# Moving the last two attention gate steps and one MLP group's norm work between pipeline turns

## The reference

```
x  = mobius_add(x, expmap0(g_msa * logmap0(attn_out)))     # the attention gate step
xm = expmap0(layer_norm(logmap0(x)) * (1 + sc_mlp) + sh_mlp)
ff = plin(plin(xm, w_f1, b_f1), w_f2, b_f2)
y  = mobius_add(x, expmap0(g_mlp * logmap0(ff)))           # the MLP gate step
out = x0 + mx_quantize(y) @ dequant(weight).T + bias       # groups of 32, FP6
```

## Time and profile before

| what | value |
|---|---|
| median of 3 runs | 1152.47 us (1149.03 to 1152.67) |
| profiled execution: its own time / its span | 1151.27 us / 1149.4 us |
| busy share of the span: PE, DVE, ACT, POOL | 87%, 84%, 74%, 48% |
| granted TensorE clock, mean over the span | 0.949 |
| loads of scale and shift rows, issue to landing (median) | 4.8 us and 5.9 us |
| first and last turn of the MLP loop touched by the change | from about 858 us to about 918 us |

### The profile page before, as it was taken

The page is one execution under the profiler, slowest core; times in us unless marked ns, Lnnn a source line. Parts: engine busy times, 40 slices in busy tenths (PEclk is TensorE's granted clock), DMA queues, the critical chain, the costliest instruction groups (busy, mean ns, idle before and its releaser), DMA issues.

```text
span 1149.4 us, 23488 instructions
## 1 busy us (share of the span) xinstructions
PE 999.6 (87%) x7666; PEld 647.6 (56%) x7688; DVE 964.9 (84%) x2211; ACT 854.4 (74%) x2322; POOL 551.0 (48%) x1009
## 2 busy tenths in 40 slices
PE   7999987887699279999999999999885688889876
PEld 7888873333355146666666666666552355455544
DVE  5888777999488867899998999999878799999983
ACT  3545548887797246888888888888778888888872
POOL 2344424554387432444444444444204576677763
PEclk9999998999599689999999999999997799999998
DMA  7111201341699643454554444442373555766634
GB/s 245 46 49 55 61 22 63 127 171 79 215 354 326 186 109 93 111 124 123 131 127 123 113 111 111 112 112 69 83 176 68 101 130 147 183 157 165 156 95 125
DMA packets 113676, 148.16 MB, mean 129 GB/s; under 512 B 9232, under 2 KB 99472, under 8 KB 112784
## 3 DMA queue, kind: packets, MB, share of 16 engines
q1 hardware_dynamic: 113008, 146.64, 46.8%
q10 hardware_dynamic: 544, 0.00, 0.0%
HBM read 111.22 MB, written 27.00 MB: 120 GB/s over the span
## 4 chain that ended last, share of the span: by engine, by line
PE 22%; issue 12%; ACT 12%; DVE 7%; POOL 6%; DMA 4%; SPq 2%; DVEq 0%; POOLq 0%; ACTq 0%
PE t_fB L2053 6%; POOL t_qk L1971 4%; PE t_bk L2022 4%; PE t_fA L2053 3%; PE t_bk L1386 3%; DMA t_qbd<-t_qt 3%; PE t_fB L1407 2%; SPq L1856 2%; ACT t_ysq L2192 1%; ACT t_junk L1425 1%; ACT t_vbd L1467 1%; ACT t_vbd L1451 1%; DVE t_qt L1619 1%; PE t_bk L2103 1%; ACT t_qt L2306 1%
## 5 line engine op out<-in xcount | busy, mean ns | idle before, releaser
L1386 PE MATMUL t_bk<-k_w12g,t_ut 128*128 128x512 f32 x256 | 126.3, 617 | 3.2 <-DVE t_y L1589 2.4
L412 POOL TENSOR_SCALAR s_hleak<-k_hs,k_leak 128x128 f32<-128x128 f32 x126 | 46.9, 372 | 96.2 <-ACT k_hs L367 96.2
L2053 PE MATMUL t_fA<-k_wqkv,t_ut 128*128 128x512 f32 (+1 forms) x256 | 91.2, 499 | 1.5 <-ACT t_ut L2162 1.5
L2053 PE MATMUL t_fB<-k_wqkv,t_ut 128*128 128x512 f32 (+1 forms) x256 | 90.9, 498 | 0.0
L285 PE MATMUL s_gsum<-k_hs,k_w0t 128*128 128x128 f32 x504 | 77.6, 297 | 6.8 <-ACT k_hs L367 0.8
L2022 PEld LDWEIGHTS t_bk<-t_qbd,t_kpar 64*128 64x128 f32 x1024 | 62.8, 189 | 31.6 <-ACT t_pt L2198 10.7
L2022 PE MATMUL t_bk<-t_qbd,t_kpar 64*128 64x128 f32 x1024 | 75.2, 287 | 6.2 <-DMA t_qbd<-t_qt 1.8
L1386 PEld LDWEIGHTS t_bk<-k_w12g,t_ut 128*128 128x128 f32 x256 | 50.4, 198 | 53.3 <-issue 49.6
L745 ACT ACTIVATE a_silu<-a_pg,k_wxscale 128x512 f32<-128x512 f32 x96 | 64.9, 694 | 17.5 <-PE a_pu L710 17.3
L285 PEld LDWEIGHTS s_gsum<-k_hs,k_w0t 128*128 128x128 f32 x504 | 65.6, 190 | 20.6 <-ACT k_hs L367 20.1
L364 ACT ACTIVATE s_gate<-s_gsum,k_b 128x128 f32<-128x128 f32 x128 | 40.1, 363 | 45.7 <-PE s_gsum L285 45.7
(11 more groups left out here) (388 smaller groups left out, 2910.1 us busy)
## 6 DMA issues: line engine op xcount, KB each, us to landing
t_scb<-g_rows SPq DMA_DIRECT2D x64, 256.0 KB, 4.8
t_shb<-g_rows SPq DMA_DIRECT2D x64, 256.0 KB, 5.9
hidden_rows<-k_own SPq DMA_DIRECT2D x6, 1536.0 KB, 6.0
t_qbd<-x_rows SPq DMA_DIRECT2D x17, 512.0 KB, 6.3
s_xrow<-in_x_dram SPq DMA_DIRECT2D x16, 512.0 KB, 3.6
b_xin<-in_x_dram SPq DMA_DIRECT2D x16, 512.0 KB, 4.5
x_rows<-b_xout SPq DMA_DIRECT2D x16, 512.0 KB, 6.6
t_xf<-x_rows SPq DMA_DIRECT2D x16, 512.0 KB, 5.6
```

Source lines behind the costliest of these rows:

```text
L1386: last = nc.tensor.matmul(z.fW[:, j, :], z.ut[:, c, j * P:(j + 1) * P], k["w12g"][:, c, :], start=False, stop=(c == C - 1))
L2053: last = nc.tensor.matmul(dst[:, w0:w1], ut[:, c, j * P:(j + 1) * P], k["wqkv"][:, c, w0:w1], start=(c == 0), stop=(c == C - 1))
```

## The change

On DVE, ACT and POOL the calls are put into another order; PE and SP are as before, and no instruction is added or taken away. The attention gate step of group 15 is issued in turn 4 on ACT and DVE (only its `gated` on DVE stays in turn 3) and at the end of turn 3 on POOL. The DVE part of group 14's step (`moved`, `moments`) goes from turn 2 to turn 3, and `squares_yo` of group 15 with POOL's `scaled_y(NG)` from turn 2 (on POOL from ahead of the loop) to turn 3. MLP group 2 has `norms_u` and `scaled_u` issued earlier in turn 2 on ACT, with `clip_u(2)` ahead of `scaled_norms(0)` on POOL and `modulate(2)`, `shift(2)` ahead of `gated(0)` on DVE. In turns other than 2, ACT's `norms_a` of the MLP stands ahead of the attention gate's `scaled_a`.

```diff
@@ POOL
             gate_step(NG)
-            scaled_y(NG)
             for i in range(NG + 4):
+                if i == 2:
+                    once(second.clip_u, 2)
                 once(second.scaled_norms, i - 2)
                 once(second.products, i - 4)
                 once(second.clip_u, i)
@@
                 once(second.quotients, i - 3)
                 once(second.factors, i - 2)
-                if i == 2:
+                if i == 3:
+                    scaled_y(NG)
                     scaled_norms(NG - 1)
+                once(second.clip_y, i - 1)
+                if i == 3:
                     gate_step(NG + 1)
-                once(second.clip_y, i - 1)
@@ ACT
-            gates = {2: turn(NG), 3: turn(NG + 1)}
+            gates = {2: turn(NG), 4: turn(NG + 1)}
@@
                 once(second.turned_u, i - 1)
                 if i in gates:
                     gates[i]["tanh_parts"]()
+                if i == 3:
+                    gates[2]["squares_yo"](NG)
+                once(second.norms_y, i - 2)
                 if i == 2:
-                    gates[i]["squares_yo"](NG)
-                once(second.norms_y, i - 2)
+                    once(second.norms_u, 2)
                 if i in gates:
                     gates[i]["inverse"]()
+                if i == 2:
+                    once(second.scaled_u, 2)
+                else:
+                    once(second.norms_a, i - 2)
+                if i in gates:
                     gates[i]["scaled_a"]()
                 once(second.norms_a, i - 2)
                 once(second.scaled_a, i - 3)
@@ DVE
-            gates = {2: turn(NG), 3: turn(NG + 1)}
+            gates = {2: turn(NG), 4: turn(NG + 1)}
@@
-                if i == 3:
-                    gates[i]["gated"]()
                 once(second.quads, i - 2)
                 once(second.moved, i - 4)
                 once(second.norm, i)
                 once(second.maxima, i - 4)
                 once(second.outer, i - 2)
+                if i == 2:
+                    once(second.modulate, 2)
+                    once(second.shift, 2)
                 once(second.gated, i - 2)
+                if i == 3:
+                    gates[2]["moved"]()
+                    gates[2]["moments"]()
+                    gates[4]["gated"]()
                 once(second.modulate, i)
                 once(second.shift, i)
-                if i in gates:
+                if i == 4:
                     gates[i]["moved"]()
                     gates[i]["moments"]()
                 once(second.gate_sums, i - 2)
```

## The result

| | before | after |
|---|---|---|
| median of 5 runs | 1152.67 us (1149.03 to 1153.08) | 1160.57 us (1158.23 to 1162.48) |
| profiled execution / span | 1151.27 / 1149.4 us | 1162.48 / 1160.7 us |
| `norm(2)` to `norm(5)` on DVE | 862.63 to 920.64: 58.01 us | 862.09 to 929.50: 67.41 us |
| from `norm(5)` to the end | 228.8 us | 231.2 us |

The changed kernel takes 1.0072 of the time before (95% interval 1.0050 to 1.0093), that is 8.3 us more. The forecast was 1161.0.

What follows compares the result with a forecast made beforehand. DVE was taken as the pace: its waits in turns 2 to 4 would grow from 8.2 to 17.1 us, 8.9 more, taking the profiled 1151.27 to 1160.2; with 1.2 for the median, the forecast was 1161.0, range 1154 to 1167.

Steps and rivals of the forecast that it cites:

- DVE is the pace: Settled MLP turn: DVE works 16.17 of 17 us, so what it loses at the transition is never caught up.
- Turn 2: DVE waits 1.6 us at quads(1) and 4.5 at outer(1) for root_quad(1), 6.1 instead of 3.8.
- Turn 3: ACT waits 1.9 us before inverse(0) for POOL's denominator; DVE runs through without a wait.
- Turn 4: Group 15: ACT waits 5.3 us before tanh_parts, 3.1 before inverse; DVE waits 11.0 at moved, starting 918.3.
- The two knots: POOL, Turn 4: scaled_norms behind quotients(0) and factors(1), gate step behind clip_y(2); ACT waits 5.3 and 3.1 us.
- The sum: DVE's waits in turns 2 to 4 total 17.1 us against 8.2, so 8.9 us more.
- The cost of a late `wide(4)`: PE may end wide(4) 0.5 to 1 us after DVE asks; offset by quads(3), so taken as nothing.
- slow-PE rival: After PE's long gap, wide(4) runs wholly at the lower clock: 6.6 us on top, 1167; 12 in 100.
- The bounds: On the 8.9 us loss: 6.1 without POOL stalls in turn 4, 0.5 without both knots; upwards, a slow PE.
- The lower bound of 0.5 us: If both POOL knots in turn 4 cost ACT nothing, the loss is 8.4 us less, 0.5.
- The 2.8 for a POOL without stalls: If DVE does not stall POOL's small instructions in turn 4, the loss is 2.8 us less, 6.1.
- The faster case: ACT's stops are filled, DVE waits under 2.1 us at group 15's moved: 2.1 us less, 1149.2; 6 in 100.

Runs made afterwards that it cites:

- before_filled: Kernel before, gates in old turns: DVE's gate_sums ahead of attention moved in turns 2 and 3, ACT's root_quad(1) and norms_a(1) earlier in turn 3; ratio 0.9999.
- both_knots: Changed kernel with POOL's scaled_y and scaled_norms of group 15 ahead of quotients(0), its gate step ahead of clip_y(2); ratio to before 1.0034.
- gate_sums_first: Changed kernel with DVE's gate_sums(2) ahead of modulate(4) and shift(4) in turn 4; ratio to the kernel before 1.0042.
- regrouped: Changed kernel with POOL as in both_knots, root_quad(1), root_quad(2), turned_u(2), norms_a(2), group 14's scaled_a earlier on ACT, gate_sums(2) earlier on DVE; ratio to before 1.0021.
- filled_and_freed: before_filled with POOL's scaled_norms of group 15 ahead of factors(0) in turn 2; ratio to the kernel before 0.9986 (0.9971 to 1.0002).
- before_dve_part: Kernel before with only DVE's gate_sums moved ahead of the attention moved in turns 2 and 3; ratio 1.0004.

## Why the prediction was right, point by point

- **DVE is the pace.** Right. The table's two columns are the evidence: stretches from -2.3 to +10.7 us come back in the times. The DVE half of before_filled marks the limit: `gate_sums` in DVE's own waits won nothing that can be seen (stretch -0.3): 1.2 us were won in turn 2, and most of that went into an instruction of DVE that now met a long one of POOL.
- **Turn 2.** `scaled_u(2)` started at 873.71 (873.7 foretold), `tanh_parts(0)` at 879.41 (879.45). DVE's stop was foretold as 1.6 at `quads(1)` and 4.5 at `outer(1)`, 6.1; it was 6.64, all at `outer(1)`. PE ran `wide(1)` at the full clock this time and had its last tile by 872.5, where the earlier trace rows have 874.7; the end, 881.2, is the same, because ACT sets it.
- **Turn 3.** ACT's wait before `inverse(0)`: 1.5 for 1.9. Nothing else waits, as written. The later loads of the gate rows cost nothing: no DMA is in the list of waits.
- **Turn 4.** Foretold and measured: ACT 5.3 and 5.5, then 3.1 and 3.2; `moved` at 918.3 and 918.16; DVE's wait 11.0 and 11.1. The two knots were then undone one at a time and gave back 5.1 and 3.1.
- **The sum.** 8.9 us forecast (as a time, 1160.2 and 1.2 make 1161.4, not the 1161.0 written); the profiled stretch grew by 9.4 and the timed difference is 8.3 (5.8 to 10.7). The cost of a late `wide(4)`, taken as nothing against the wait that falls away at `quads(3)`, was fair: `quads(3)` and `quads(4)` follow each other by 15.4 us, with no wait. The list in the earlier trace rows ends at 918; at 918.45 DVE waited 0.57 us in `quads(3)` for the last tile of `wide(3)`, so the slow products of the old order did cost DVE something, against what the slow-PE rival says. That is the wait that falls away.
- **The bounds.** The lower bound of 0.5 us, both knots costing ACT nothing, was added up from two waits that overlap: both_knots is 3.8 us above before in the stretch and 3.9 in time, with 3.2 of ACT's wait left. The 2.8 for a POOL without stalls stands for three instructions; gate_sums_first freed two of them, and ACT's wait fell by 1.7.
- **The slow PE.** The long gap came, the price did not. `turn_xd(0)` waited 12.4 us and its eight transposes took 1.94, but by `mixed(0)` four products took 1.03 and `wide(4)` ran at 1.88 per tile throughout:

```profile
925.31 1.94 PE L1398 MATMUL t_fB<-k_ident,t_qbd 128*128 128x128 f32 x8 [12.38 <-POOL t_qbd L1351]
...
928.86 1.03 PE L1407 MATMUL t_fB<-k_wmt,t_qbd 128*128 128x256 f32 x4
...
933.44 1.88 PE L1386 MATMUL t_bk<-k_w12g,t_ut 128*128 128x512 f32 x4 [0.62 <-DVE t_y L1589]
```

- **The faster case** named what it would need: DVE's wait at group 15's `moved` under 2.1 us. With both knots undone it is 5.3 and the kernel 3.9 us slower than before, so even the repaired form of this change doesn't reach it.

## What to carry to other kernels

In a pipeline written out by hand, moving a step one turn later is not only moving its work: walk the step's handshakes on each queue and ask what now stands ahead of each half. Here ACT came to wait for a small product behind POOL's `quotients`, which itself waits for this turn's DVE work, and POOL for an ACT result that the gate step did not need. And an engine that gets earlier brings its long instructions onto its neighbour's short ones: before_filled lost its gain so, and regrouped a part of it; filled_and_freed got it back, in the stretch, by putting first the instructions that someone waits for. The same meeting also costs the other side: DVE's instructions of 0.17 and 1.32 us took 1.90 and 2.03 beside POOL's of 1.91. It shows in no list of waits, only in a duration, so compare durations between kernels too.

## What the runs showed that I had not expected

The settled turns are not alike from one execution to the next. From `norm(5)` to the end the profiled executions take 228.8 us (before) to 234.8 us (before_dve_part), with no order that the timed ratios follow. In the changed kernel's profile two settled turns cost DVE 2.3 and 1.7 us in waits for `wide`, where PE had come back from a wait of 2.3 to 2.7 us at the lower level of its clock. The same wait does not always cost it: in this profile `turn_u` took 1.94 us behind one of 2.30 (at 1045.00) and 1.06 behind one of 2.31 (at 1077.14). Here the first of the two turns, four products of `mixed` each time:

```profile
1013.44 1.91 PE L1407 MATMUL t_fB<-k_wmt,t_qbd 128*128 128x256 f32 x4
...
1017.21 1.03 PE L1407 MATMUL t_fB<-k_wmt,t_qbd 128*128 128x256 f32 x4
```

Granted clock and the rest from 925 to 1140 us, columns as in the earlier trace rows, in the kernel before and in the changed one:

```profile
925.00:1140.00 215.00, 179.47 (x716) 110.79 (x726) 191.69 (x492) 173.17 (x627) 149.10 (x277) 0.96 0.59 148
```

```profile
925.00:1140.00 215.00, 183.24 (x708) 113.96 (x721) 193.76 (x508) 176.50 (x637) 148.80 (x290) 0.93 0.57 143
```

Of the 11.3 us by which the profiled spans differ, 9.4 lie in the stretch and 2.4 behind it; the medians differ by 7.9, and the changed kernel's profiled execution is the slowest of its five. How many such turns an execution draws would explain the spread of its times (1158.2 to 1162.5), but only one execution of each kernel was profiled, so that is argued and not shown.
